# A clamp moved from ScalarE into VectorE's second pass over attention scores

## The reference

```python
E = exp(clip(-mu * |ti - tj|, -30, 0))              # decay, one per head
s = einsum('bihd,bjhd->bhij', qr, conj(kr)).real    # rotated queries and keys
qn, kn = |q|^2 , |k|^2                              # row norms and key norms
V = sigma_sq / (2 mu) * (1 - E*E) + (eta_sq + gamma_sq)
maha = maximum(qn[..., None] + (E*E) * kn - 2 E * s, 0) / V
logits = coef * log1p(maha / nu) - 0.5 * DH * log(V)
A = softmax(where(causal, logits, -inf));  out = A @ v;  y = out @ Wo
```

## Time and profile before

| what | value |
| --- | --- |
| median of three runs | 1684.14 us |
| profiled execution | 1685.38 us |
| its span | 1683.6 us |
| TensorE busy | 1624.1 us (96%) |
| VectorE busy | 1494.5 us (89%) |
| ScalarE busy | 1443.1 us (86%) |
| GpSimd busy | 1013.6 us (60%) |
| granted TensorE clock | 0.999 of full |

### The profile page before, as it was taken

How to read it: one execution, slowest core, us unless ns; L and a number is a source line. 1 busy time by engine, 2 the same in 40 slices (tenths; PEclk the granted TensorE clock), 3 DMA queues, 4 the chain that set the end, 5 groups by cost and what they waited for, 6 DMA issues and landing times. The chain is left out here.

```text
span 1683.6 us, 31247 instructions
## 1 busy us (share of the span) xinstructions
PE 1624.1 (96%) x9690; PEld 1227.8 (73%) x9690; DVE 1494.5 (89%) x3380; ACT 1443.1 (86%) x2909; POOL 1013.6 (60%) x954
## 2 busy tenths in 40 slices
PE   5999988999999999999999999999999999899998
PEld 4787865777776777677777777777776776677876
DVE  6878878999999999999999999999999989977665
ACT  6677678999999999999999999999999998765765
POOL 3564556666666666665766666666666656245555
PEclk9999999999999999999999999999999999999999
DMA  6000022232223323232222323232232322100000
GB/s 178 1 1 1 1 97 73 64 92 64 76 70 76 79 64 85 58 82 70 75 74 64 92 64 76 55 92 69 74 84 60 80 59 51 26 8 7 13 13 13
DMA packets 50484, 100.05 MB, mean 59 GB/s; under 512 B 8208, under 2 KB 25872, under 8 KB 50320
## 3 DMA queue, kind: packets, MB, share of 16 engines
q1 hardware_dynamic: 50320, 98.07, 22.7%
HBM read 17.95 MB, written 5.24 MB: 14 GB/s over the span
## 5 line engine op out<-in xcount | busy, mean ns | idle before, releaser
L1500 POOL TENSOR_TENSOR early<-early 128x1024 f32<-128x1024 f32 x127 | 303.7, 2391 | 421.4 <-PE pS L1191 227.6
L661 POOL TENSOR_TENSOR hid_lo_d<-hid_d,hid_hi_d 128x512 fp32r<-128x512 f32 x176 | 231.4, 1315 | 218.4 <-ACT hid_hi_d L566 211.8
L1392 ACT ACTIVATE early<-early,qnorm 128x128 f32<-128x128 f32 (+3 forms) x512 | 246.6, 552 | 68.0 <-DVE early L1591 67.3
L1191 PE MATMUL pS<-early 128*128 128x128 f32 (+3 forms) x1024 | 297.6, 433 | 0.4 <-PEq L115 0.4
L1376 ACT ACTIVATE early<-early,nmax 128x128 f32<-128x128 f32 (+3 forms) x512 | 280.9, 558 | 7.7 <-DVE nmax L1578 7.4
L1191 PEld LDWEIGHTS pS<-early 128*128 128x128 f32 x1024 | 164.7, 191 | 96.1 <-issue 61.4
L1587 DVE SCALAR_TENSOR_TENSOR pS<-pS,ek 128x1280 f32<-128x1280 f32 x128 | 190.9, 1492 | 43.5 <-PE pS L1191 41.9
L1509 POOL TENSOR_TENSOR ek<-early 128x128 f32<-128x128 f32 (+3 forms) x256 | 216.1, 877 | 3.0 <-ACT early L1384 2.6
L1509 POOL TENSOR_TENSOR ek<-decay,early 128x128 f32<-128x128 f32 (+3 forms) x256 | 215.0, 873 | 0.0
L1233 PE MATMUL pS<-ident,early 128*128 128x128 f32 x1280 | 184.9, 278 | 13.3 <-DVE early L1591 7.0
L1405 ACT ACTIVATE early<-early,params 128x512 f32<-128x512 f32 (+1 forms) x256 | 196.4, 816 | 0.0
(11 more groups left out here) (393 smaller groups left out, 3752.5 us busy)
## 6 DMA issues: line engine op xcount, KB each, us to landing
early<-early SPq DMA_DIRECT2D x263, 256.0 KB, 3.4
early<-trig_d SPq DMA_DIRECT2D x64, 64.0 KB, 2.0
trig_d<-early SPq DMA_DIRECT2D x3, 1024.0 KB, 6.9
early<-in_w SPq DMA_DIRECT2D x3, 704.0 KB, 8.7
x_sb<-in_x SPq DMA_DIRECT2D x4, 512.0 KB, 8.3
early<-in_wqk SPq DMA_DIRECT2D x16, 128.0 KB, 3.4
cos<-trig_d SPq DMA_DIRECT2D x32, 64.0 KB, 2.2
sin<-trig_d SPq DMA_DIRECT2D x32, 64.0 KB, 2.0
```

Source lines behind the costliest of these rows:

```text
L661: g.tensor_tensor(hid_lo[:, par], hid[:, par], hid_hi[:, par].bitcast(F32), ALU.subtract).then_inc(lo_done, 1)
L1191: last = pe.matmul(s.pS[:, span(I)], rot[:, I * P:(I + 1) * P], rot[:, N:N + (I + 1) * P], start=True, stop=True)
L1392: last = a.activation(u[:, span(I)], u[:, span(I)], ACT.Relu, bias=qnorm[:, r % 2, I:I + 1])
L1500: g.tensor_tensor(rot[:], by_cos[:], crossed[:], ALU.add).then_inc(S["rot_done"], 1)
```

## The change

The second pass becomes four instructions, for each row tile one, that add `ek` and cap the sum from above at 3e38 and from below at `low`, a value for each row. The first pass now multiplies the scores by -2 and by the decay. For that, `ek` is now the squared decay times the key norm, where it was the decay times the key norm. The rectifier on ScalarE goes, and the logarithm becomes four instructions with a bias for each row (`base`), the row norm less a constant plus a lower bound. GpSimd makes `base`, `floor` and `low` with three small dependent instructions where it made `qnorm` with one. The spread now waits for the second pass of the pair before, the expansion of the decay for the first pass, and the squared decay gets two more buffers for even heads. To make room for them, the low part of the second dense weights is stored to memory in the first dense part and loaded back near the end of the attention part, both from GpSimd's queue; the second dense part waits for it.

```diff
+LEAST = 2.0 ** -21
...
 # first and second dense part
+                if last_phase and e == 0:
+                    pe.wait_ge(s.S["w2_back"], 16)
...
                 down_low(1)
+                g.wait_ge(w2_lo, len(PIECES2))
+                g.dma_start(s.w2_low_d, s.w2s[1][:]).then_inc(s.S["w2_kept"], 16)
...
 # SyncE, expand(h)
-                wait(sp, S["t_done"], 2 * (h - 1) * B)
+                wait(sp, S["w_done"], (h - 1) * B)
...
 # ScalarE
-            def clamp(i, r):
-                n = i * 16 + r
-                wait(a, S["qn_done"], n + 1)
-                for k, (_, pieces) in enumerate(HALVES):
-                    wait(a, S["t_done"], 2 * n + k + 1)
-                    for I in pieces:
-                        last = a.activation(u[:, span(I)], u[:, span(I)], ACT.Relu, bias=qnorm[:, r % 2, I:I + 1])
-                    last.then_inc(S["relu_done"], 1)
...
-                for k, (half, _) in enumerate(HALVES):
-                    a.wait_ge(S["relu_done"], 2 * n + k + 1)
-                    a.activation(u[:, half], u[:, half], ACT.Ln, bias=hp(h, U_MIN)).then_inc(S["ln_done"], 1)
+                a.wait_ge(S["qn_done"], n + 1)
+                for k, (_, pieces) in enumerate(HALVES):
+                    a.wait_ge(S["t_done"], 2 * n + k + 1)
+                    for I in pieces:
+                        last = a.activation(u[:, span(I)], u[:, span(I)], ACT.Ln, bias=base[:, r % 2, I:I + 1])
+                    last.then_inc(S["ln_done"], 1)
...
                 if live(i, r):
-                    clamp(i, r)
+                    logs(i, r)
                 if live(i, r - 1):
                     turned_out(i, r - 1)
-                if live(i, r):
-                    logs(i, r)
...
 # GpSimd
-                wait(g, S["decay_done"], i * 2 + r // B + 1)
-                wait(g, expanded[par], 48 * (i + r // 16 + 1) if par else 64 * (i + r // 16))
+                wait(g, S["decay2_done"], h + 1)
                 wait(g, S["norm_done"], n + 1)
-                wait(g, S["w_done"], n)
+                wait(g, S["t_done"], 2 * n)
                 for I in ORDER:
-                    last = g.tensor_tensor(ek[:, span(I)], decay[par][:, span(I)], knorm[:, 0:(I + 1) * P], ALU.mult)
+                    last = g.tensor_tensor(ek[:, span(I)], decay2(h)[:, near(I)], knorm[:, 0:(I + 1) * P], ALU.mult)
...
+            def restore():
+                g.wait_ge(S["ek_done"], (H - 1) * B)
+                g.wait_ge(S["lnv_done"], H - 1)
+                g.wait_ge(S["av_done"], (H - 1) * B)
+                g.dma_start(s.w2s[1][:], s.w2_low_d).then_inc(S["w2_back"], 16)
...
-                g.tensor_scalar(qnorm[:, r % 2, :], column, hp(h, NEG_NU_A), None, ALU.subtract).then_inc(S["qn_done"], 1)
+                at_ = base[:, r % 2, :], floor[:, r % 2, :], low[:, r % 2, :]
+                g.tensor_scalar(at_[0], column, hp(h, NEG_NU_A), hp(h, U_MIN), ALU.subtract, ALU.add).then_inc(S["base_done"], 1)
+                g.wait_ge(S["base_done"], n + 1)
+                g.tensor_scalar(at_[1], at_[0], LEAST, hp(h, U_MIN), ALU.mult, ALU.max).then_inc(S["floor_done"], 1)
+                g.wait_ge(S["floor_done"], n + 1)
+                g.tensor_tensor(at_[2], at_[1], at_[0], ALU.subtract).then_inc(S["qn_done"], 1)
...
 # VectorE, distances(i, r)
-                wait(v, S["s_done"], n + 1)
-                wait(v, S["ek_done"], n + 1)
-                v.scalar_tensor_tensor(s.pS[:, 0:SW], s.pS[:, 0:SW], -2.0, ek[:], ALU.mult, ALU.add).then_inc(S["w_done"], 1)
-                wait(v, S["w_done"], n + 1)
+                v.wait_ge(S["decay_done"], i * 2 + r // B + 1)
+                wait(v, expanded[par], 48 * (i + 1) if par else 64 * i)
+                v.wait_ge(S["s_done"], n + 1)
+                v.scalar_tensor_tensor(s.pS[:, 0:SW], s.pS[:, 0:SW], -2.0, decay[par][:, 0:SW],
+                                       ALU.mult, ALU.mult).then_inc(S["w_done"], 1)
+                v.wait_ge(S["w_done"], n + 1)
+                v.wait_ge(S["ek_done"], n + 1)
+                v.wait_ge(S["qn_done"], n + 1)
                 wait(v, S["zred_done"], 2 * n)
-                for half, _ in HALVES:
-                    v.tensor_tensor(u[:, half], s.pS[:, half], decay[par][:, half], ALU.mult).then_inc(S["t_done"], 1)
+                for _, pieces in HALVES:
+                    for I in pieces:
+                        last = v._custom_dve(bass.dve_ops.TENSOR_ADD_SAT, out=u[:, span(I)], in0=s.pS[:, span(I)],
+                                             in1=ek[:, span(I)], s0=HIGHEST, s1=low[:, r % 2, I:I + 1])
+                    last.then_inc(S["t_done"], 1)
```

More of the change, by code:

```diff
@@ L1050, in attention_phase @@
         sem = lambda name: ctx.enter_context(nc.semaphore(name))
+        square_even = tuple(sb(f"square_even{k}", [P, N])[:] for k in range(2))
+        val_even = [sb(f"val_even{k}", [P, N]) for k in range(3)]
         decay = (s.decay0, sb("decay1", [P, SW]))
@@ L1056, in attention_phase @@
         wqk = (s.wqk0, [sb(f"wqk1_{half}", [P, 2 * P], F32R) for half in ("hi", "lo")])
-        decay2, wqk_raw, by_cos, by_sin, crossed = s.decay2, s.wqk_raw, s.by_cos, s.by_sin, s.crossed
+        wqk_raw, by_cos, by_sin, crossed = s.wqk_raw, s.by_cos, s.by_sin, s.crossed
         squares, rot, knorm, u, z = s.squares, s.rot, s.knorm, s.u, s.z
-        qnorm = sb("qnorm", [P, 2, TILES])
-        q_turned = sb("q_turned", [P, 2, P])
+        base, floor, low = (sb(n, [P, 2, TILES]) for n in ("base", "floor", "low"))
+        q_turned = s.dist[:, 2 * N:SW].rearrange("p (k d) -> p k d", k=2)
         ek = sb("ek", [P, SW])
         probT = [sb(f"probT{k}", [P, SW]) for k in range(2)]
-        val_even = [sb(f"val_even{k}", [P, N]) for k in range(3)]
         val_odd = [sb(f"val_odd{b}", [P, N]) for b in range(B)]
@@ L1087, in far, with decay2 @@
             return decay[h % 2][:, span(TILES - 1)] if h % 2 or h == 0 else s.far_even
+        def decay2(h):
+            return s.decay2 if h % 2 else square_even[h // 2 % 2]
         def hp(h, k):
@@ L1514, in query_norms @@
                 wait(g, S["qt_done"], n + 1)
-                wait(g, S["relu_done"], 2 * (n - 1))
+                wait(g, S["ln_done"], 2 * (n - 1))
                 column = q_turned[:, r % 2].rearrange("p (c d) -> p c d", c=TILES)[:, :, 0]
-                g.tensor_scalar(qnorm[:, r % 2, :], column, hp(h, NEG_NU_A), None, ALU.subtract).then_inc(S["qn_done"], 1)
+                at_ = base[:, r % 2, :], floor[:, r % 2, :], low[:, r % 2, :]
[4 more added lines that the diff above has]
+                g.tensor_tensor(at_[2], at_[1], at_[0], ALU.subtract).then_inc(S["qn_done"], 1)
             def a_step(i, r):
@@ L1526, in a_step @@
                     build_first()
+                if i * 16 + r == (H - 1) * B + 3:
+                    restore()
             steps(nc.gpsimd, a_step)
@@ L1532, in build_front @@
             def build_front(h):
-                if h % 2:
-                    wait(v, S["norm_done"], (h - 1) * B)
-                else:
+                if h % 2 == 0:
                     wait(v, expanded[0], 64 * (h // 2 - 1))
@@ L1556, in build_square @@
                 v.wait_ge(S["lnv_done"], h)
-                v.tensor_tensor(decay2[:], far(h), far(h), ALU.mult).then_inc(S["decay2_done"], 1)
+                wait(v, S["ek_done"], (h - (1 if h % 2 else 3)) * B)
+                v.tensor_tensor(decay2(h), far(h), far(h), ALU.mult).then_inc(S["decay2_done"], 1)
             def build_back(h):
@@ L1794, in program @@
         s = Shared(args, out)
+        s.w2_low_d = nc.dram_tensor("w2_low_d", [P, HC * P], F32R, kind="Internal").ap()
         s.trig_d = nc.dram_tensor("trig_d", [3, H, DH // 2, N], F32, kind="Internal").ap()
@@ L1799, in program @@
         s.w13 = [sb(f"w13_{h}", [P, 2 * HC * P], F32R) for h in ("hi", "lo")]
-        s.w2s = [sb(f"w2_{h}", [P, HC * P], F32R) for h in ("hi", "lo")]
+        w2_hi = sb("w2_hi", [P, HC * P], F32R)
         s.wr = sb("wr", [P, 2 * NE], F32R)
@@ L1839, in program @@
         s.xn1 = part(2 * N).rearrange("p (j q t) -> p j q t", j=2, q=TILES)
-        at[0] = SW
+        at[0] = SW + N
         s.var1, s.root1, s.rstd1, s.shift1 = (part(TT) for _ in range(4))
@@ L1848, in program @@
         s.silu1 = part(2 * N).rearrange("p (a t) -> p a t", a=2)
-        dense_phase(nc, s, 0)
+        w2_low = lambda n: nc.sbuf_tensor(f"w2_lo{n}", [P, HC * P], F32R)
+        with w2_low(0) as first:
+            s.w2s = (w2_hi, first)
+            dense_phase(nc, s, 0)
+        with w2_low(1) as again:
+            s.w2s = (w2_hi, again)
         attention_phase(nc, s)
-        dense_phase(nc, s, 1)
+        with w2_low(2):
+            dense_phase(nc, s, 1)
 def kernel(**inputs):
```

13 lines of the change are left out of this document (7 added, 6 removed).

## The result

The changed kernel takes 1741.76 us (median of four runs, 1741.08 to 1742.18), beside 1685.22 us before (median of four runs): ratio 1.0336, 95% interval 1.0319 to 1.0354. It is 56.5 us slower; 42 were forecast, and the range reached to 1765.

The account below looks back on a forecast made before the run. Even steps were taken as bound by a closed VectorE and TensorE chain, odd ones by VectorE with TensorE close behind. 1685.38 + 20.5 (even) + 20.5 (odd) + 1 (transfers) = 1727.4, so median 1726; range 1700 to 1765.

Parts of the forecast that it names:

- The bound of either kind of step: Even steps: a closed chain of VectorE's passes and TensorE, 9.87 us; odd: VectorE, 8.84 us, TensorE close behind at 8.55.
- Second pass, +0.28 for pieces: VectorE's second pass: four instructions instead of two lengthen it by 0.28 us in each step.
- The waits before it, +0.04: Before VectorE's second pass: two more satisfied waits, for the spread and GpSimd's small results, cost 0.04 us, bounds 0 and 0.2.
- First pass: 0: VectorE's first pass: same operation, widths and kinds of operands, its wait for the expanded decay met, so no cost.
- The logarithm's hole, -0.22: Odd steps: the peaks wait 0.22 us for ScalarE's logarithm after the reciprocal; the earlier logarithm removes this.
- The collision, +0.37: Odd steps: the later spread and three small GpSimd instructions overlap VectorE's peaks, costing 0.37 us per step.
- Even steps, the late spread: 0: Even steps: VectorE's idle time takes up the later spread's overlap, so it costs nothing.
- Rival A: Odd steps: small GpSimd instructions and the spread's end stop the peaks in full, 1.39 us; total 1793; chance 0.16.
- Rival B: Cheap second-pass instructions, and spread and peaks interleave: odd steps fall to 8.77, total 1696; chance 0.19.
- D: How much later the second pass ends in each step: forecast 0.32 us, bounds 0.22 and 0.6.
- Rival C: The four second-pass pieces stream as one and closing the logarithm's hole pays: odd steps 8.60, total 1673; chance 0.08.
- The weights' transfers, +1: Storing and reloading 704 KB of weights from GpSimd's queue delays a spread at most: 1 us, bounds 0 and 9.

Follow-up runs that it names:

- b1: Kernel before, with the plain second pass in four pieces instead of two, nothing else: 1700.73 us, ratio 1.0092.
- a2: Changed kernel with the second pass in two custom pieces with pointers, the exact bound for each row left out: 1711.85 us, ratio 1.0163 to before.
- c1: Changed kernel with the second pass's lower bound a constant 1.0 instead of a pointer for each row, four pieces kept: 1714.17 us, ratio 1.0172 to before.
- b3: Kernel before without the rectifier (clamp left out), the logarithm in four biased pieces in its place: 1680.67 us, ratio 0.9977.
- a1: Changed kernel with VectorE's first pass waiting for the scores ahead of the two decay waits: 1736.02 us, ratio 1.0306 to before.
- d1: Kernel before with the first pass's two waits swapped, the spread's first and the scores' last: 1690.11 us, ratio 1.0032.
- a5: Changed kernel with both the wait for the scores first and a second `ek` buffer for three of four pieces: 1722.91 us, ratio 1.0222 to before.
- a4: Changed kernel with a second `ek` buffer for three of four pieces, so the spread starts earlier: 1735.11 us, ratio 1.0303 to before.
- b2: Kernel before with the spread released by the second pass of the pair before instead of the first: 1693.76 us, ratio 1.0046.
- c2: Changed kernel with the scores' wait first, two second-pass pieces and a constant bound (row's own bound left out): 1693.16 us, ratio 1.0049 to before.
- a3: Changed kernel with one small GpSimd instruction instead of three, the lower bound a constant pointer: 1743.41 us, ratio 1.0351 to before.
- d2: Kernel before, computation whole, with the logarithm's first half moved ahead of ScalarE's copy of the turned probabilities: 1676.17 us, ratio 0.9952.

## Why the prediction was right, and where it was off

- *The bound of either kind of step.* Right. Whatever lengthened the second pass (b1, a2, c1) moved the even step by the same amount, and TensorE's odd chain, put at 8.55 from one gap, is the shortest odd step of b3.
- *Second pass, +0.28 for pieces.* Right mechanism, mis-sized: 0.37, which is 2 x 0.065 for instructions and 4 x 0.06 for pointers. The folds that I took as the low end carry a pointer themselves, and I counted their surplus for the two added instructions only, while the pointer is new in all four. 128 x 0.09 = 12 us, of the 14.6 by which the change was forecast short (41.9 against 56.5). The 0.36 for two more instructions, worked out from the fixed part of a duration, is out: b1 shows 0.13.
- *The waits before it, +0.04.* Nothing: the second pass starts 1.52 after the first in both kernels.
- *First pass: 0.* This step failed. I looked at operands and at whether the waits are met, and not at which of them is met last and where it stands. a1 and d1 move the even step by 0.09, a5 against a4 by 0.12: about 6 us. That the waits before the second pass cost nothing where 5 us were put down hid this by luck.
- *The logarithm's hole, -0.22.* Right as a wait: the peaks start at 6.42 after the first pass instead of 6.27 + 0.37, and b3 shows the cause. But it is no gain of its own beside a late spread, as b2 and c2 show: the 0.22 come back as a longer collision, and of the prediction's two terms only the sum, 0.15, can be read.
- *The collision, +0.37.* Right: 2.31 instead of 1.96 for the peaks of an ordinary step, and with late steps 2.33 against 2.09 on the mean. The share for the small instructions (0.05) was nothing (a3). An ordinary odd step was put at 9.16 and takes 9.18. On the mean the odd step has 0.37 from the second pass, -0.23 from the hole and 0.24 from the peaks, together 0.38, found 0.39.
- *Even steps, the late spread: 0.* Nearly right: VectorE's idle time takes it, but for the eighth step of most even heads (10.47 beside 10.35), about 1 us in all. Three single even steps of heads 2 to 14 took 10.55 to 10.70; what lengthened them stays open.
- *Rival A*, VectorE shut out by each small instruction: out by a3. The rows of a3 show GpSimd waiting for running peaks, those of b3 the peaks waiting for a running spread. By the rule of the Trainium skill (SBUF — State Buffer, "SBUF: two separate sides") whichever of the two starts first keeps the ports for its whole instruction. The rows agree in who waits, not quite in the length: held until the spread's recorded end, the first of the peaks would end at 847.82 + 0.32 = 848.14, and it ended at 847.97. My rival had let each small one stop the peaks for its full 0.30, and the later peaks of a step keep their 0.61 and 0.47 beside them.
- *Rival B* (D = 0.22): its price for an instruction (0.11) was even too high; what it lacked is the price of a pointer in all four. *Rival C*: without pieces and pointers, with the wait in front, the rest of the change (c2) still costs 0.5%, so it would not have been faster: with a spread that late, the hole pays nothing. It does pay with the early spread, as d2 shows.
- *The weights' transfers, +1.* Outside the attention part the time changed by 1.4 us behind it and -0.8 ahead of it (first pass of pair 0 at 260.0, of pair 127 at 1510.3).

The account sums: regular steps 56 x 0.51 + 56 x 0.39 = 50.4, the first and the last head 2.5 and 3.2, together 56.1 us in the attention part; the spans differ by 56.6.

## What to carry to other kernels

Work taken off an engine that is in no closed chain pays only through what waits for it, and where it stood it may have kept two others apart: find the step's chain first, then count each added instruction and each per-row pointer on it. An engine that starts earlier meets another one earlier, so look for what runs there. And where several waits precede an instruction, put the one that is met last in front: the same waits in another order were worth 0.3%.

## What the runs showed of the hardware that I had not expected

- On VectorE a further instruction over the same columns cost 0.065 us, a pointer to a value for each row as scalar operand 0.06 us, and the custom operation nothing beyond the plain product (two plain pieces 1.55, two custom ones with constants 1.55, four plain 1.68, four custom with constants 1.68, two custom with pointers 1.68, four with pointers 1.93).
- VectorE's first pass, which waits for several semaphores, started 0.04 us after the end of the scores in the profile when the wait for them stood first, and 0.12 to 0.15 when it stood last.
- The spread on GpSimd stretched VectorE's peaks (0.35 to 0.68) and also a conversion with one SBUF input (0.26 to 0.71); running peaks stretched a small GpSimd instruction (0.30 to 0.82).
- Late landings of the rotation's transfer (5.1 to 5.5 instead of 4.3 us after the end of the product that feeds it, in some odd steps, without another transfer in flight in most of them) lengthen steps in nearly every version; d2 has hardly any. Their cause stays open.
